# VectorE adds the causal masks of three query blocks of a group instead of two

## The reference, cut to what matters

```python
q = (x @ wq).reshape(b, s, NH, HD)
k = (x @ wk).reshape(b, s, NKV, HD)
v = (x @ wv).reshape(b, s, NKV, HD)
k = jnp.repeat(k, NREP, axis=2)
v = jnp.repeat(v, NREP, axis=2)
scores = jnp.einsum('bihd,bjhd->bhij', q, k) * SCALE
causal = jnp.tril(jnp.ones((s, s), dtype=bool))
scores = jnp.where(causal, scores, jnp.finfo(scores.dtype).min)
attn = jax.nn.softmax(scores, axis=-1)
out = jnp.einsum('bhij,bjhd->bihd', attn, v)
```

## Time and profile before

| | us |
|---|---|
| median of 3 runs | 929.34 (927.82 to 931.89) |
| the profiled execution | 929.51 |
| its span, first to last instruction | 927.7 |
| PE busy | 859.9 (93%) |
| DVE busy | 681.3 (73%) |
| ACT busy | 532.0 (57%) |
| POOL busy | 192.9 (21%) |

### The profile page before, as it was taken

How to read it: one execution, slowest core, us unless ns; L and a number is a source line. 1 busy time by engine, 2 the same in 40 slices (tenths; PEclk the granted TensorE clock), 3 DMA queues, 4 the chain that set the end, 5 groups by cost and what they waited for, 6 DMA issues and landing times.

```text
span 927.7 us, 13672 instructions
## 1 busy us (share of the span) xinstructions
PE 859.9 (93%) x5096; PEld 679.2 (73%) x5096; DVE 681.3 (73%) x1066; ACT 532.0 (57%) x707; POOL 192.9 (21%) x199
## 2 busy tenths in 40 slices
PE   3798999999979798998999999999988999999996
PEld 1466777777657687776888888788866888888885
DVE  3745888888879687787778786577796866667842
ACT  3412767777553544686666666576647767666820
POOL 3002566668755034100000000000120000000004
PEclk9798999999989999999999999999999999999998
DMA  9588578887750022114333333132312433332202
GB/s 312 170 251 168 54 100 136 137 129 93 152 172 1 34 69 81 46 52 138 99 105 105 106 101 114 37 101 91 114 41 69 118 104 94 99 91 77 60 1 91
DMA packets 38450, 95.35 MB, mean 103 GB/s; under 512 B 7144, under 2 KB 10216, under 8 KB 37360
## 3 DMA queue, kind: packets, MB, share of 16 engines
q1 hardware_dynamic: 34256, 89.11, 39.6%
q10 hardware_dynamic: 4128, 5.36, 1.7%
HBM read 79.56 MB, written 2.21 MB: 88 GB/s over the span
## 4 chain that ended last, share of the span: by engine, by line
PE 58%; DVE 7%; ACT 3%; issue 2%; POOL 2%; DMA 1%; POOLq 0%; SPq 0%; DVEq 0%; ACTq 0%
PE PS L1611 13%; PE PS L1613 13%; PE PS L1612 13%; PE PS L1924 5%; PE PS L1926 5%; PE PS L1925 5%; POOL X L780 2%; DVE SCR L1217 1%; DVE ST L1159 1%; DVE ACC L1232 1%; PE PS L1907 1%; PE PS L1895 1%; DVE FQ L1325 1%; PE PS L1854 1%; DMA WF<-in_LBGU 1%
## 5 line engine op out<-in xcount | busy, mean ns | idle before, releaser
L903 ACT ACTIVATE PL<-CODE 128x1024 f32<-128x1024 int32 x200 | 202.4, 1057 | 59.7 <-DVE ACC L1232 57.1
L1611 PE MATMUL PS<-HH,WRH 128*128 128x512 f32 x448 | 176.7, 394 | 11.6 <-DVE HL L1191 5.1
L1612 PE MATMUL PS<-HH,WRL 128*128 128x512 f32 x448 | 175.6, 392 | 0.0
L1613 PE MATMUL PS<-HL,WRH 128*128 128x512 f32 x448 | 175.3, 391 | 0.0
L780 POOL TENSOR_TENSOR X<-X,SCR 128x512 f32<-128x512 f32 x32 | 42.6, 1348 | 567.9 <-DVE SCR L1217 567.8
L1232 DVE SCALAR_TENSOR_TENSOR ACC<-PL,ACC 128x1024 f32<-128x1024 f32 x100 | 123.8, 1238 | 9.4 <-DVE ACC L1232 1.4
L951 ACT ACTIVATE PT<-PS 128x512 f32<-128x512 f32 x160 | 86.4, 604 | 46.4 <-PE PS L1729 25.0
L797 POOL TENSOR_TENSOR QS<-ident,MX 64x256 fp32r<-64x256 f32 x128 | 97.9, 765 | 57.5 <-DVE MX L1391 36.9
L1611 PEld LDWEIGHTS PS<-HH,WRH 128*128 128x128 f32 x448 | 84.8, 189 | 31.6 <-issue 6.3
L1613 PEld LDWEIGHTS PS<-HL,WRH 128*128 128x128 f32 x448 | 84.8, 189 | 17.9
L1612 PEld LDWEIGHTS PS<-HH,WRL 128*128 128x128 f32 x448 | 85.0, 190 | 16.8
(11 more groups left out here) (230 smaller groups left out, 1517.1 us busy)
## 6 DMA issues: line engine op xcount, KB each, us to landing
CODE<-in_CODES SPq DMA_DIRECT2D x50, 512.0 KB, 3.5
SCALE<-in_SCALES SPq DMA_DIRECT2D x100, 256.0 KB, 4.0
WM<-in_WM SPq DMA_DIRECT2D x12, 1024.0 KB, 5.6
QS<-FQ SPq DMA_DIRECT2D x32, 256.0 KB, 6.4
X<-in_X ACTq DMA_DIRECT2D x2, 1024.0 KB, 12.6
KS<-KHL SPq DMA_DIRECT2D x32, 64.0 KB, 5.3
KN<-KHL SPq DMA_DIRECT2D x32, 64.0 KB, 4.6
GAB<-gates SPq DMA_DIRECT2D x4, 512.0 KB, 3.9
```

The costliest lines, as they stand in the source:

```text
L903: nc.scalar.activation(PL[:, n % 3], CODE[:, p % 2], ACT.Prelu, scale=scale, bias=bias, alpha=alpha).then_inc(s_plane, 1)
L1611: nc.tensor.matmul(dst, lh, rh, start=start and k == 0, stop=False)
L1612: nc.tensor.matmul(dst, ll, rh, start=False, stop=False)
L1613: ins = nc.tensor.matmul(dst, lh, rl, start=False, stop=stop and k == KC - 1)
```

## The change

One constant is changed. For block 2 of each of the 16 groups the mask products of the scores (L1716) are no longer issued, and VectorE takes that block's maxima with four `tensor_tensor_reduce` of 384 columns in place of two `reduce_max` of 768. `CMASK` is as before; its last 384 columns are used for that block. The products at L1732 stay, and block 3 is as before.

```diff
-ADDED_MASK = (0, 1)
+ADDED_MASK = (0, 1, 2)
```

## The result

The changed kernel takes **931.85 us** (median of 16 runs, 929.80 to 932.57) where the kernel before, beside it, takes 929.50 (16 runs, 927.46 to 933.04). The ratio is 1.0024 [1.0013, 1.0035], so the change costs 1.2 to 3.3 us. Forecast were 931.7 us and 2.25 us more. The profiled execution took 932.57 us, against 929.51 before.

The account below looks back on a forecast made before the run. The attention was taken as a loop in which VectorE and TensorE wait for each other in turn. 1.36 + 0.69 + 0.20 = 2.25 us on 929.51 gave 931.8, forecast 931.7 us; range for 8 in 10, 926.5 to 934.8.

Parts of the forecast that it names:

- VectorE's price: Block 2 on VectorE: four 384-column instructions take 2.03 us where two reductions took 1.74, 0.29 us more per block.
- TensorE's saving: Block 2's scores: 64 products are 3.8 us, but only the first pair's readiness counts, 0.12 us earlier.
- VectorE's groups: Eight groups where VectorE runs without a gap from block 2 on: 0.17 us longer each, 1.36 us in all.
- the term 0.17: Group's lengthening on VectorE's path: 0.29 us more in block 2 less the 0.12 us earlier start.
- TensorE's groups: Three groups where block 3's second pair waits for block 2's second pair: TensorE 0.23 us later, 0.69 us in all.
- The wait that I named: TensorE before block 3's second pair, until block 2's second pair is reduced: path 2.23 us, less 0.12 for the earlier start.
- Cover by a decoding sum: Two groups with a decoding sum behind block 3: TensorE 0.23 us late, 0.13 to spare, 0.10 each, 0.20 in all.
- ScalarE's groups: Three groups where block 3 waits for ScalarE's exponential: that wait covers the 0.17 us, so nothing is added.
- TensorE is the bound: Rival: TensorE's products in the attention were the loss; 1.9 to 3.8 us faster, middle 926.7 us; chance 0.18.
- No cover: Rival: every group pays VectorE's whole 0.29 us for block 2, 4.6 us more, 934.1 us; chance 0.18.
- The condition that the prediction gives for the first rival: TensorE's 0.23 us delay must fall under its 0.12 gain, so block 2's four instructions take under some 1.9 us.
- The clock falls more often: Rival: TensorE's longer attention waits, some 0.4 us a group, lower the clock; one spell 933.5 us, three 937; chance 0.12.

Follow-up runs that it names:

- `(1,)`: Kernel before with block 0 also back on mask products and two reductions, only block 1 masked on VectorE: 927.16 us, ratio 0.9965.
- pair 1 alone: Kernel before with only the second pair of heads of block 2 masked on VectorE, the first keeping its products: 931.45 us, ratio 1.0030.
- the moved kernels: GpSimd's scaling and additions two units later, in the kernel before (931.53 us), with the change (932.31) and with only block 1 masked on VectorE (930.82).
- the moved change: Changed kernel with GpSimd's scaling and adding of decoded codes two units later: 932.31 us, ratio 1.0022 against the kernel before.
- the kernel before with the move: Kernel before with GpSimd's scaling and adding of decoded codes two units later: 931.53 us, ratio 1.0022.
- `(1,)` with the move: Kernel before with only block 1 masked on VectorE and GpSimd's scaling and additions two units later: 930.82 us, ratio 1.0010.

## Why the prediction was right, and which terms were off

**VectorE's price: right.** The straight line through two shapes gave 0.52 us a step and 2.03 a block; measured 0.51 to 0.52 and 2.02. The 384-column form has no price of its own. That what costs is the fixed part of each instruction agrees with `(1,)`, where two reductions in place of four instructions on block 0 save 0.36 us each in groups 2, 6 and 10.

**TensorE's saving: right in kind, small in size.** The first pair is ready 0.15 to 0.16 us earlier where I had 0.12. The removal of the products alone gives 0.15 to 0.18 where VectorE or TensorE sets the pace.

**VectorE's groups: the term 0.17 is 0.13.** 0.29 - 0.16 = 0.13, and six groups show 0.11 to 0.15. The term was over-sized by the earlier start alone. Group 0, with 0.02, was counted wrongly as one without a gap: VectorE waits before its block 3 in both profiles, 0.49 us before (at 91.49) and 0.38 now (at 92.06), which covers 0.11. Group 14, partly at half clock, shows 0.06; I have not separated why. In all 0.85 for 1.36.

**TensorE's groups: right.** 0.19 and 0.15 for 0.23, which the earlier start makes 0.19, and 0.32 in the last one, whose end is another event. The wait that I named, before block 3's second pair, grew from 0.18 to 0.35. The run with pair 1 alone shows that this pair is the whole price: groups 1 to 14 without 5 and 8 are 1.56 us longer there and 1.53 in the change.

**Cover by a decoding sum: under-sized.** 0.18 and 0.19 for 0.10. The prediction had VectorE's list on time. In group 9, counted from block 2's start, the sum begins 0.17 later (4.24 to 4.41 us), while GpSimd's addition, which stands behind the diagonals of block 2's last maximum, ends 0.35 later (4.62 to 4.97). They overlap by 0.18 more, and the sum lasts 0.17 longer. Starting 0.17 later and lasting 0.17 longer, less the 0.15 by which the next block 2 is ready earlier, makes the 0.19. The step of the prediction that had these groups wait for TensorE's 0.23 did not happen: VectorE's list, taken to be on time, sets them. That GpSimd's operation is what lengthens it is shown by the moved kernels (1.22, and 1.85 to 2.27 elsewhere). The Trainium skill states the mechanism, "SBUF — State Buffer", section "Who interferes with whom": a VectorE instruction with two SBUF inputs and a GpSimd instruction that reads SBUF exclude each other, and the later one stands until the other is through. Here both lengths agree with it, some 0.13 us apart: 0.38 + 1.22 = 1.60 for 1.47, and 0.56 + 1.22 = 1.78 for 1.64. The moved kernels agree by the same 0.13 to 0.15: 0.78 + 1.22 for 1.85, 1.19 + 1.22 for 2.27, and 0.87 + 0.68 for the division's 1.42.

**ScalarE's groups: right twice, wrong once.** Groups 5 and 13 are unchanged to 0.01, their wait for ScalarE being longer now (1.00 us in group 5 in place of 0.58). Group 8 is 0.39 longer. VectorE's timeline there, changed kernel:

```profile
176.69 0.69 DVE L1318 TENSOR_TENSOR NUM<-NUM,DENS 128x512 f32<-128x512 f32 x1
177.93 2.35 DVE L1391 TENSOR_REDUCE MX<-PS 128x2 f32<-128x1024 f32 x2 [0.56 <-DVE NUM L1318]
```

And TensorE's, first the wait for ScalarE, then the product that completes the first pair:

```profile
176.12 0.50 PE L1729 MATMUL PS<-QS,KN 128*128 128x512 f32 x1 [0.90 <-ACT PT L951]
...
177.26 0.22 PE L1716 MATMUL PS<-maskR,padR 128*128 128x128 f32 x1
```

In the kernel before, TensorE's wait is 0.46 and the reduction starts 0.32 us after that product (175.75 to 176.07). Now it starts 0.67 after it, one head later. The same 0.67 to 0.69 stands at this place in the run with the four instructions and the products (178.74 to 179.42) and in the moved change, and 0.31 to 0.32 where only the products or only one pair is changed. I found no wait in the code that would explain it; it stays open, and it is 0.35 of the 2.25 us.

So the total agrees with the forecast to 0.1 us by terms of which one is 0.5 too large and two are together 0.5 too small. The sign and the order of size are founded; the last tenth is luck.

**The rivals.** *TensorE is the bound* falls: without its products the kernel is at most 2.1 us faster, and both pairs would have cost the same. *No cover* falls in the complete change, where 0.13 of 0.29 is paid, and is what the run with products kept shows, with some 0.3 in nearly every group. The condition that the prediction gives for the first rival doesn't follow from its sum: with block 2 at 1.9 us TensorE would still be 0.10 late, and only under 1.80 would its 0.23 be gone. *The clock falls more often* is not seen in the attention of the changed kernel: one stretch of 0.66, at 250 in place of 246. Behind the attention its profile has more of the lower level, as told above, but its 16 runs have a granted clock of 0.976 in the median, as the kernel before has. TensorE's timeline before the stretch:

```profile
248.90 1.00 PE L1713 MATMUL PS<-KS,QS 128*128 128x256 f32 x4 [1.87 <-DVE MX L1387]
```

Its chance of 0.12 was not idle: the one profile with all four blocks on VectorE has two new stretches, and lacks the one near the end.

## What to carry to other kernels

When two engines wait for each other in turn, price a trade on the path round the loop: here 3.8 us of TensorE's work bought 1.55 us, because only what makes the first pair ready earlier counts, and 0.29 us per block of VectorE's work cost 0.13 to 0.19. The same trade had another sign in another block (with block 1 on VectorE it pays, with 0 and 2 it doesn't, though for block 0 the stretch at half clock is most of the difference), so it is worth trying place by place, and per half of a block. A shift of 0.2 us also moves what runs beside the shifted work: look for pairs of VectorE and GpSimd operations that overlap already.

## What the runs showed of the chip that I had not expected

**Short waits before half clock.** The stretches at the lower level follow TensorE's waits of 1.74 us, 1.87 (the changed kernel), and 1.06 and 1.07 (all four blocks on VectorE). But three waits as long were followed by full clock: 1.73 (the kernel before with the move), 1.74 (`(1,)` with the move) and 2.09 (all four blocks). TensorE's timeline and the windows view of the first of these:

```profile
249.32 1.00 PE L1713 MATMUL PS<-KS,QS 128*128 128x256 f32 x4 [1.73 <-DVE MX L1387]
...
249.00:254.00 5.00, 4.68 (x44) 3.70 (x45) 3.73 (x17) 3.07 (x6) 3.72 (x5) 1.00 0.91 188
```

So the wait just ahead does not decide it alone; what does stays open. The Trainium skill, "TensorE: Matmul & The Clock Gate", section "Why this matters for your kernels", warns of idle gaps longer than any of these; these traces do not agree, since the level fell after shorter ones. One stretch costs 1.5 to 1.9 us by the length of its group, as much as the whole change on ten groups.

**A sum beside GpSimd.** The same VectorE instruction, 1024 columns and two inputs in SBUF, takes 1.21 to 1.22 us where no GpSimd instruction is under way at its start, also where one starts during it. Where one is under way for another 0.18 to 1.19 us, it takes 1.26 to 2.28: in all these cases of the twelve profiles its length is that remainder plus 1.08 us, to 0.01.

**A DMA beside the loop.** The reciprocal in group 5 waits for the DMA of the softmax sums 1.26 us with pair 1 alone, 1.09 with `(1,)`, 0.59 with the products kept, and no more than 0.05 in the kernel before and the changed one. The edits don't touch it, so a single group's length can hold such a wait.

**The attention's start.** With the code ahead of it identical, the attention began anywhere from 82.7 to 86.1 us in the profiles of these kernels. Differences of under two microseconds between two single profiles must be read inside the stage, group by group, and not off the span.
